# A mixture-of-experts loop: gate and up product as three fp32r products of high and low parts

## The chip, the cores and the metric

The kernel runs on one core of a Trainium2 chip. The metric is the device time of one execution in microseconds (us), start of the program to its end. The engines are PE (TensorE, matrix products, with a queue of weight loads of its own, PEld), ACT (ScalarE), DVE (VectorE), POOL (GpSimd) and SP (SyncE, which here issues most transfers). Each runs its own list of instructions in order; they meet at semaphores. SBUF is the on-chip memory of 128 partitions, PSUM the memory that PE writes its products to. TensorE's clock has two levels, 2.4 GHz (a granted clock of 1.00 in the rows) and 1.2 GHz (0.50).

## The reference

A decoder of two layers on 2 x 1024 tokens of 256 values. The change touches the last part alone, the experts of the second layer. What they compute, cut to that:

```python
xn = layernorm(x, gamma, beta); xf = xn.reshape(2048, 256)
probs = clip(softmax(xf @ router_w.T), 1e-8, 1.0)
topk_p, topk_i = top_k(probs, 2)              # two of 8 experts for each token
for eid in range(8):
    xe = xf * dense_gate[:, eid:eid + 1]      # scaled rows
    gate, up = split(xe @ gate_up_w[eid].T, 2)    # 256 -> 2 x 512
    out = out + (silu(gate) * up) @ down_w[eid].T # 512 -> 256
x = layernorm(x + xn + out)
```

All is float32.

## The kernel before, in words

The kernel is a chain of stages: chunked attention, cross attention, the mxfp4 layer, causal attention, a second cross attention, and `stage_experts` (L2088). The weights of all experts lie in SBUF when the last stage begins (`ExpertWeights`, L2072): `gate_up` of 8 x 2 x 1024 columns, `down` of 8 x 4 x 256.

`stage_experts` has three blocks. The first normalises the tokens, writes them to DRAM (`xn_rows`), routes them, and sorts the 4096 choices into slots of 128 rows, each of one expert: 39 slots (`SLOT_TILES`, L57), whose expert numbers are in `expert`. It ends with two one-hot matrices on DVE (L2367) and the products `tile_values` on POOL (L2236) and DVE (L2380), from which PE sums the slots' tables (L2277).

The second block is the experts' loop (L2396 to L2511). Each engine has a `step` function, which `lagged` (L92) calls once a slot: it gives the step the number of the newest slot and of the slots one, two or more behind it, so that in one step an engine works on several slots. With `turns=True` it also passes the turn modulo 4. In a step

- POOL (L2404) multiplies the gathered rows of slot t by their gates (L2410), copies the next slot's token indices (L2415) and issues its gather (L2418), then, for the slot three behind t, copies the choice indices (L2423) and issues the scatter of the output rows (L2426). Each issue waits for the copy in front of it.
- PE (L2440) transposes the hidden rows of slot u2 (L2447), makes the gate and up product of slot u1 (L2454), transposes the rows of slot t (L2462), and makes the down product of u2 (L2468).
- ACT (L2478) applies Silu to the gate half of u1 (L2482), copies the transposed rows of t out of PSUM (L2487), and the output rows of u2 (L2492).
- DVE (L2499) copies the transposed hidden rows of u2 (L2504) and multiplies gate by up for u1 (L2509).

There is one buffer for each of these intermediate tiles; the order within a step is written out by hand, and a semaphore counts the slots for each. The gate and up product of 128 rows is four matmuls in float32, of two halves of 512 columns and two halves of 128 contraction rows each:

```python
for n in range(2):
    for k in range(KD):
        last = nc.tensor.matmul(core.ps_s[:, n * FF:(n + 1) * FF], rows_tr[:, k, :],
                                weights.gate_up[:, bass.ds(x, 1), k, n * FF:(n + 1) * FF]..., start=(k == 0), stop=(k == KD - 1))
```

In the trace a float32 matmul stands as two records, an fp32r matmul (the type float32r, which PE takes in one pass) as one. The number x of the slot's expert is read by PE's queue from SBUF into a register (`value_load`, L2437).

The third block adds the two output rows of each token and normalises.

Of the kernel before, what the change touches and what calls it, by code (L numbers as in the profile page):

```python
# [28 lines left out]
P = 128  # L29
# [2058 lines left out]
def stage_experts(core, weights):  # L2088
# [17 lines left out]
    with core.stage() as ctx:  # L2106
        scratch = core.shared[:].rearrange("p (t d) -> p t d", d=D)
        router = core.sb(ctx, "ex_router", [P, KD, EXPERTS])
        gamma_row, beta_row = (core.sb(ctx, f"ex_{n}_row", [P, D]) for n in ("gamma", "beta"))
# [3 lines left out]
        xn_tr = [core.sb(ctx, f"ex_xn_tr{i}", [P, BATCHED, KD, P]) for i in range(2)]  # L2113
# [14 lines left out]
        past = core.sb(ctx, "ex_past", [P, SLOT_COLUMNS, EXPERTS])  # L2128
# [7 lines left out]
        in_tile = core.sb(ctx, "ex_in_tile", [P, 2, TILES, SLOT_COLUMNS])  # L2136

        gate_parts = core.sb(ctx, "ex_gate_parts", [P, 2, 2, TILES])
        tile_values = core.sb(ctx, "ex_tile_values", [P, 2, TILES, 3, SLOT_COLUMNS], F32R)
# [3 lines left out]
        at_place = core.sb(ctx, "ex_at_place", [P, TILES, P], F32R)  # L2143
# [22 lines left out]
        rows_tr_ready, rows_tr_copied, gate_up_ready = sem("rows_tr_ready"), sem("rows_tr_copied"), sem("gate_up_ready")  # L2166
# [228 lines left out]

        with nc.Block() as block:  # L2396
# [35 lines left out]
            @block.tensor  # L2432
            def _(pe):
                pe.wait_ge(weights.loaded, 16 * weights.LOADS)

                def expert_of(s):
                    return pe.value_load(expert[0:1, s:s + 1] if isinstance(s, int) else expert[0:1, bass.ds(s, 1)],  # L2437
                                         min_val=0, max_val=EXPERTS - 1)

                def step(t, u1, u2):  # L2440

                    x, y = (None if i is None else expert_of(i) for i in (u1, u2))
                    if u2 is not None:
                        pe.wait_ge(hidden_ready, u2 + 1)
                        need(pe, hidden_tr_copied, u2)
                        for k in range(KF):
                            last = nc.tensor.transpose(core.ps_c[:, k * P:(k + 1) * P], hidden[:, k * P:(k + 1) * P], core.ident[:])  # L2447
                        last.then_inc(hidden_tr_ready, 1)
                    if u1 is not None:

                        pe.wait_ge(rows_tr_copied, u1 + 1)
                        for n in range(2):
                            for k in range(KD):
                                last = nc.tensor.matmul(core.ps_s[:, n * FF:(n + 1) * FF], rows_tr[:, k, :],  # L2454
                                                        weights.gate_up[:, bass.ds(x, 1), k, n * FF:(n + 1) * FF].rearrange("p a n -> p (a n)"),
                                                        start=(k == 0), stop=(k == KD - 1))
                        last.then_inc(gate_up_ready, 1)
                    if t is not None:
                        pe.wait_ge(row_ready, t + 1)
                        need(pe, rows_tr_copied, t)  # L2460
                        for k in range(KD):
                            last = nc.tensor.transpose(core.ps_q[:, k * P:(k + 1) * P], row[:, k * P:(k + 1) * P], core.ident[:])  # L2462
                        last.then_inc(rows_tr_ready, 1)
                    if u2 is not None:
                        pe.wait_ge(hidden_tr_copied, u2 + 1)
                        need(pe, down_copied, u2)
                        for k in range(KF):
                            last = nc.tensor.matmul(core.ps_y[:, 0:D], hidden_tr[:, k, :],  # L2468
                                                    weights.down[:, bass.ds(y, 1), k, :].rearrange("p a n -> p (a n)"),
                                                    start=(k == 0), stop=(k == KF - 1))  # L2470
                        last.then_inc(down_ready, 1)

                lagged(pe, SLOT_TILES, 2, step)

            @block.scalar
            def _(act):

                def step(t, u1, u2):  # L2478
# [15 lines left out]
                lagged(act, SLOT_TILES, 2, step)  # L2494

            @block.vector
            def _(dve):

                def step(t, u1, u2):  # L2499
                    if u2 is not None:  # L2500
# [10 lines left out]
                lagged(dve, SLOT_TILES, 2, step)  # L2511

# [158 lines left out]
```

## Time and profile before

| what | value |
|---|---|
| runs | 1430.58 us median of 3 (1429.42 to 1432.01) |
| the profiled execution | 1428.61 us, span 1426.9 us |
| mean granted clock | 0.93 |
| PE busy | 1213.3 us (85%) |
| PEld busy | 846.1 us (59%) |
| DVE busy | 779.6 us (55%) |
| ACT busy | 668.0 us (47%) |
| POOL busy | 583.1 us (41%) |
| gate/up records on PE (L2454) | 312, 143.4 us busy |
| down records on PE (L2468) | 312, 73.9 us busy |

The span runs from the first to the last instruction. The experts' loop lies between 1144 and 1386 us of it. A record's length on PE is modelled, and records overlap: how fast PE goes is to be read from the distance of their starts.

### The profile page before, as it was taken

How to read it: one execution, taken by the hardware profiler on the slowest of the kernel's cores; microseconds unless marked ns; L12 is line 12 of the kernel's file. 1: busy time of each engine (PE TensorE's matmuls, PEld its weight loads, DVE VectorE, ACT ScalarE, POOL GpSimd, SP SyncE). 2: the span in 40 equal slices, each digit the busy share in tenths (PEclk: the TensorE clock that was granted, in tenths of full speed). 3: DMA queues.
4: the chain of work that ended last, by engine and by line, in shares of the span. 5: the costliest groups of instructions: out<-in, count | busy, mean ns of one | idle time of the engine just before them, and what ended most of it. 6: DMA issues, size and time to landing. Idle time of an engine off the chain costs nothing. (4 is left out here: it accounts for less than half of the span.)

```text
span 1426.9 us, 24233 instructions
## 1 busy us (share of the span) xinstructions
PE 1213.3 (85%) x7903; PEld 846.1 (59%) x7904; DVE 779.6 (55%) x1427; ACT 668.0 (47%) x1967; POOL 583.1 (41%) x664
## 2 busy tenths in 40 slices
PE   7888589565999999999899999998984279999970
PEld 4544367454666767776666777766764246666640
DVE  2587799783345556563455566656876612222215
ACT  2588357344556556655555566643661012222212
POOL 1255357557335324313643222102664245555535
PEclk9999689896899999999999999999995579999995
DMA  9000000010011010001100001007202001111105
GB/s 304 25 1 1 0 1 2 1 30 16 16 31 29 3 31 16 16 2 31 28 19 16 16 2 45 2 1 284 71 1 68 0 30 45 48 44 47 45 29 177
DMA packets 36134, 56.02 MB, mean 39 GB/s; under 512 B 6528, under 2 KB 27392, under 8 KB 36032
## 3 DMA queue, kind: packets, MB, share of 16 engines
q1 hardware_dynamic: 32288, 44.47, 10.5%
q0 software_dynamic: 3744, 10.23, 2.2%
q8 instruction: 59, 0.97, 0.3%
q14 instruction: 43, 0.35, 0.1%
HBM read 34.90 MB, written 9.31 MB: 31 GB/s over the span
## 5 line engine op out<-in xcount | busy, mean ns | idle before, releaser
L2016 DVE TENSOR_REDUCE ga_neg_top<-ps 128x1 f32<-128x128 f32 (+7 forms) x256 | 182.1, 753 | 195.0 <-PE ps L1786 194.6
L1897 ACT ACTIVATE ga_e<-ps,ga_neg_top 128x128 f32<-128x128 f32 (+7 forms) x256 | 188.2, 743 | 7.5 <-DVE ga_neg_top L2016 6.8
L1906 ACT COPY ga_e_tr<-ps 128x512 f32<-128x512 f32 (+3 forms) x192 | 92.1, 479 | 174.3 <-PE ps L1795 171.4
L1795 PE MATMUL ps<-ident,ga_e 128*128 128x128 f32 x1152 | 165.2, 279 | 0.9 <-DVE ga_e_tr L2024 0.8
L1811 PE MATMUL ps<-ga_e_tr,ga_v 128*64 128x256 f32 x1152 | 151.7, 391 | 4.1 <-ACT ga_att L1914 4.1
L2454 PE MATMUL ps<-ex_gate_up,shared 128*128 x312 | 143.4, 603 | 0.5 <-ACT shared L2487 0.5
L1795 PEld LDWEIGHTS ps<-ident,ga_e 128*128 128x128 f32 x1152 | 123.3, 142 | 28.1 <-ACT ga_e L1897 14.7
L2024 DVE COPY ga_e_tr<-ps 128x128 f32<-128x128 f32 (+3 forms) x192 | 106.0, 552 | 35.0 <-PE ps L1795 34.7
L1971 POOL TENSOR_TENSOR ga_q_lo<-shared,ga_q_hi 128x1024 fp32r<-128x1024 f32 x15 | 35.5, 2369 | 175.6 <-ACT ga_q_hi L1887 175.6
L2509 DVE TENSOR_TENSOR shared<-shared,ps 128x512 f32<-128x512 f32 x39 | 26.8, 687 | 137.0 <-ACT shared L2482 137.0
L1811 PEld LDWEIGHTS ps<-ga_e_tr,ga_v 128*64 128x64 f32 x1152 | 72.4, 136 | 49.0 <-issue 23.3
L2454 PEld LDWEIGHTS ps<-ex_gate_up,shared 128*128 128x128 f32 x312 | 57.3, 194 | 58.6 <-issue 58.6
L818 POOL TENSOR_TENSOR xa_e<-xa_e,xa_recip 128x1024 f32<-128x1024 f32 x32 | 60.9, 1902 | 69.7 <-DVE xa_recip L938 69.7
L2482 ACT ACTIVATE shared<-ps 128x512 f32<-128x512 f32 x39 | 23.3, 597 | 137.6 <-PE ps L2454 137.6
L1783 PE MATMUL ps<-ga_k_hi,ga_q_hi 64*128 64x512 f32 (+3 forms) x384 | 79.3, 409 | 4.1 <-PEq L158 2.3
L493 ACT ACTIVATE ca_e<-ps,ca_neg_top 128x64 f32<-128x64 f32 x256 | 75.9, 360 | 0.2 <-DVE ca_neg_top L524 0.2
L2468 PE MATMUL ps<-ex_down,shared 128*128 x312 | 73.9, 380 | 1.0 <-DVE shared L2504 1.0
L1957 POOL TENSOR_TENSOR shared<-shared,ga_cos 128x1024 f32<-128x1024 f32 x18 | 42.7, 2370 | 74.8 <-DMA shared<-shared 71.0
L1247 PE MATMUL ps<-x_tr,wide_weights 128*128 128x128 f32 x512 | 66.9, 286 | 2.0 <-ACT ga_e_tr L1906 2.0
L1783 PE MATMUL ps<-ga_k_lo,ga_q_hi 64*128 64x512 f32 (+3 forms) x384 | 67.7, 348 | 0.0
L1783 PE MATMUL ps<-ga_k_hi,ga_q_lo 64*128 64x512 f32 (+3 forms) x384 | 67.6, 348 | 0.0
L1247 PEld LDWEIGHTS ps<-x_tr,wide_weights 128*128 128x128 f32 x512 | 62.7, 200 | 8.2 <-issue 5.8
(321 smaller groups left out, 2533.8 us busy)
## 6 DMA issues: line engine op xcount, KB each, us to landing
shared<-shared SPq DMA_DIRECT2D x80, 128.0 KB, 2.4
ex_gate_up<-in_ex_gate_up SPq DMA_DIRECT2D x1, 8192.0 KB, 24.5
ex_down<-in_ex_down SPq DMA_DIRECT2D x1, 4096.0 KB, 35.8
x_tr<-in_x_tr SPq DMA_DIRECT2D x4, 512.0 KB, 7.0
x_nat<-in_x SPq DMA_DIRECT2D x1, 2048.0 KB, 11.7
xn_rows<-x_tr SPq DMA_DIRECT2D x8, 256.0 KB, 2.1
x_tr<-choice_rows SPq DMA_DIRECT2D x8, 256.0 KB, 5.0
shared<-choice_rows SPq DMA_DIRECT2D x8, 256.0 KB, 5.7
```

Source lines behind the costliest of these rows:

```text
L493: last = nc.scalar.activation(e[buffer][:, keys], ps_scores[buffer][:, keys], ACT.Exp, scale=SCALE, bias=neg_top[buffer][:, m:m + 1], accu ...
L818: nc.gpsimd.tensor_tensor(rows, rows, recip[:].unsqueeze(2).to_broadcast(by_head), ALU.mult).then_inc(weights_ready, 1)
L1247: last = nc.tensor.matmul(bank[:, g * P:(g + 1) * P], wq[:, k, block_of], x_tr[:, k, J * P:(J + 1) * P], start=(k == 0), stop=(k == KD - 1))
L1783: nc.tensor.matmul(ps_scores(t, half)[:, k0:k1], qs[J % 2][rows, c * R + r, :], ks[slot][rows, c, 0:k1 - k0], start=(i == 0), stop=(i == 2 ...
L1795: last = nc.tensor.transpose(ps_tr[n % 2][:, (kb - k0) * P:(kb - k0 + 1) * P], e[half][t % 2][:, kb * P:(kb + 1) * P], core.ident[:])
L1811: last = nc.tensor.matmul(ps_att[half * HD:(half + 1) * HD, :], v[:, v_slot(b, kb), kv * HD:(kv + 1) * HD], e_tr[g % 2][:, kb, half, :], s ...
L1897: nc.scalar.activation(e[half][t % 2][:, 0:blocks(t) * P], ps_scores(t, half), ACT.Exp, bias=neg_top[t % 2][:, half:half + 1], accum_out=s ...
L1906: nc.scalar.copy(e_tr[g % 2][:, k0:k1, half, t % 2 * P:(t % 2 + 1) * P], ps_tr[n % 2][:, 0:(k1 - k0) * P].rearrange("p (k t) -> p k t", t= ...
L2016: nc.vector.tensor_reduce(neg_top[t % 2][:, half:half + 1], ps_scores(t, half), AX.X, ALU.max, negate=True).then_inc(top_ready, 1)
L2024: nc.vector.tensor_copy(e_tr[g % 2][:, k0:k1, half, t % 2 * P:(t % 2 + 1) * P], ps_tr[n % 2][:, 0:(k1 - k0) * P].rearrange("p (k t) -> p k ...
L2454: last = nc.tensor.matmul(core.ps_s[:, n * FF:(n + 1) * FF], rows_tr[:, k, :], weights.gate_up[:, bass.ds(x, 1), k, n * FF:(n + 1) * FF].r ...
L2468: last = nc.tensor.matmul(core.ps_y[:, 0:D], hidden_tr[:, k, :], weights.down[:, bass.ds(y, 1), k, :].rearrange("p a n -> p (a n)"), start ...
```

## The change

The gate and up product is made as three fp32r products, high rows by high weights, high rows by low weights, low rows by high weights: 12 matmuls of 512 columns. The weights of the slot's expert are split in each step, one slot ahead: ACT copies them to `w_hi` in fp32r, DVE subtracts that from the weights to `w_lo`; there are two buffers of each, taken in turn. The transposed rows are split in the same way, by ACT's copy out of PSUM and a subtraction on DVE. The product's semaphore is split in two, after the gate half and after the up half. ACT and DVE read the slot's expert number themselves. To make room, buffers that only the first block uses are given back before the loop.

```diff
-        rows_tr = flat[:, 0:D].rearrange("p (k t) -> p k t", k=KD)
...
+        front_ctx.close()
+        loop_ctx = ExitStack()
+
+        def expert_at(engine, s):
+            return engine.value_load(expert[0:1, s:s + 1] if isinstance(s, int) else expert[0:1, bass.ds(s, 1)],
+                                     min_val=0, max_val=EXPERTS - 1)
+
+        w_hi, w_lo = ([core.sb(loop_ctx, f"ex_w_{n}{i}", [P, KD, 2 * FF], F32R) for i in range(2)] for n in ("hi", "lo"))
+        rows_hi, rows_lo = (core.sb(loop_ctx, f"ex_rows_{n}", [P, KD, P], F32R) for n in ("hi", "lo"))
...
     PE
                     if u1 is not None:
-                        pe.wait_ge(rows_tr_copied, u1 + 1)
-                        for n in range(2):
-                            for k in range(KD):
-                                last = nc.tensor.matmul(core.ps_s[:, n * FF:(n + 1) * FF], rows_tr[:, k, :],
-                                                        weights.gate_up[:, bass.ds(x, 1), k, n * FF:(n + 1) * FF].rearrange("p a n -> p (a n)"),
-                                                        start=(k == 0), stop=(k == KD - 1))
-                        last.then_inc(gate_up_ready, 1)
+                        buffer = (turn - 1) % 2
+                        pe.wait_ge(rows_lo_ready, u1 + 1)
+                        pe.wait_ge(w_lo_ready, KD * (u1 + 1))
+                        for n, ready in ((0, gate_half_ready), (1, gate_up_ready)):
+                            columns = slice(n * FF, (n + 1) * FF)
+                            for i, (rows, w) in enumerate(((rows_hi, w_hi), (rows_hi, w_lo), (rows_lo, w_hi))):
+                                for k in range(KD):
+                                    last = nc.tensor.matmul(core.ps_s[:, columns], rows[:, k, :], w[buffer][:, k, columns],
+                                                            start=(i == 0 and k == 0), stop=(i == 2 and k == KD - 1))
+                            last.then_inc(ready, 1)
                     if t is not None:
                         pe.wait_ge(row_ready, t + 1)
-                        need(pe, rows_tr_copied, t)
+                        need(pe, rows_lo_ready, t)
...
     ACT
+                def step(t, u1, u2, turn):
+                    if t is not None:
+                        x = expert_at(act, t)
+                        need(act, gate_up_ready, t - 1)
+                        for k in range(KD):
+                            nc.scalar.copy(w_hi[turn % 2][:, k, :], weights.gate_up[:, bass.ds(x, 1), k, :]
+                                           .rearrange("p a n -> p (a n)")).then_inc(w_hi_ready, 1)
                     if u1 is not None:
-                        act.wait_ge(gate_up_ready, u1 + 1)
+                        act.wait_ge(gate_half_ready, u1 + 1)
...
-                        nc.scalar.copy(rows_tr, core.ps_q[:, 0:D].rearrange("p (k t) -> p k t", k=KD)).then_inc(rows_tr_copied, 1)
+                        nc.scalar.copy(rows_hi[:], core.ps_q[:, 0:D].rearrange("p (k t) -> p k t", k=KD)).then_inc(rows_hi_ready, 1)
...
     DVE (behind the copy of hidden_tr)
+                    if t is not None:
+                        x = expert_at(dve, t)
+                        need(dve, gate_up_ready, t - 1)
+                        for k in range(KD):
+                            dve.wait_ge(w_hi_ready, KD * t + k + 1)
+                            nc.vector.tensor_tensor(w_lo[turn % 2][:, k, :], weights.gate_up[:, bass.ds(x, 1), k, :].rearrange("p a n -> p (a n)"),
+                                                    w_hi[turn % 2][:, k, :].bitcast(F32), ALU.subtract).then_inc(w_lo_ready, 1)
                     if u1 is not None:
                         dve.wait_ge(gate_ready, u1 + 1)
+                        dve.wait_ge(gate_up_ready, u1 + 1)
...
                         nc.vector.tensor_tensor(hidden, act_gate, core.ps_s[:, FF:2 * FF], ALU.mult).then_inc(hidden_ready, 1)
+                    if t is not None:
+                        dve.wait_ge(rows_hi_ready, t + 1)
+                        nc.vector.tensor_tensor(rows_lo[:], core.ps_q[:, 0:D].rearrange("p (k t) -> p k t", k=KD), rows_hi[:].bitcast(F32),
+                                                ALU.subtract).then_inc(rows_lo_ready, 1)
```

POOL's step is unchanged.

## Rows read from the trace of the kernel before

**Rows 1.** Busy time by stretch: from:to, length, busy us (instructions) of five engines, granted clock, DMA.

```profile
1200.00:1225.00 25.00, 25.00 (x94) 15.19 (x93) 6.10 (x9) 4.93 (x12) 12.99 (x23) 1.00 0.14 46
1150.00:1158.00 8.00, 6.86 (x10) 2.78 (x10) 0.43 (x1) 2.27 (x4) 2.82 (x4) 0.61 0.08 24
920.00:940.00 20.00, 20.00 (x156) 14.51 (x154) 11.94 (x14) 10.79 (x19) 0.00 (x0) 1.00 0.01 2
1135.00:1143.00 8.00, 4.55 (x21) 4.19 (x20) 3.18 (x6) 0.00 (x0) 0.00 (x0) 0.50 0.00 0
1085.00:1100.00 15.00, 11.73 (x56) 11.36 (x57) 14.79 (x21) 2.92 (x5) 8.57 (x7) 0.50 0.29 99
```

**Rows 2.** Timeline of one slot: start us, length us, engine, line, operation.

```profile
1239.85 0.60 PE L2447 MATMUL ps<-ident,shared 128*128 128x128 f32 x4
1240.13 0.37 ACT L2492 COPY shared<-ps 128x256 f32<-128x256 f32 x1 [1.08 <-PE ps L2468]
1240.29 3.60 PE L2454 MATMUL ps<-ex_gate_up,shared 128*128 x8
1240.64 0.69 DVE L2504 COPY shared<-ps 128x512 f32<-128x512 f32 x1 [1.14 <-PE ps L2447]
...
1243.72 0.38 PE L2462 MATMUL ps<-ident,shared 128*128 128x128 f32 x2
1243.92 0.60 ACT L2482 ACTIVATE shared<-ps 128x512 f32<-128x512 f32 x1 [3.42 <-PE ps L2454]
1244.55 0.69 DVE L2509 TENSOR_TENSOR shared<-shared,ps 128x512 f32<-128x512 f32 x1 [3.23 <-ACT shared L2482]
```

**Rows 3.** Timeline of POOL around the same slot.

```profile
1238.53 0.61 POOL L2410 TENSOR_TENSOR shared<-shared,ex_slot_gate 128x256 f32<-128x256 f32 x1 [0.96 <-PE ps L2462]
...
1242.38 1.01 POOL L2426 DMA_INDIRECT choice_rows<-shared,ex_tile_choice  x1 [0.82 <-POOL ex_tile_choice L2423]
1244.35 0.61 POOL L2410 TENSOR_TENSOR shared<-shared,ex_slot_gate 128x256 f32<-128x256 f32 x1 [0.96 <-PE ps L2462]
```

**Rows 4.** Timeline of PE and its loads: scores, router, slot sums, first slot.

```profile
932.59 0.39 PE L1783 MATMUL ps<-ga_k_hi,ga_q_lo 64*128 64x512 f32 x2
932.82 0.40 PE L1783 MATMUL ps<-ga_k_lo,ga_q_hi 64*128 64x512 f32 x2
...
1090.05 1.83 PEld L2259 LDWEIGHTS ps<-ex_router,ex_xn_tr 128*128 128x128 f32 x8
...
1138.26 3.49 PEld L2277 LDWEIGHTS ps<-ex_tile_values,ex_at_place 128*128 128x128 f32 x16 [2.56 <-DVE ex_at_place L2367]
...
1150.27 6.64 PE L2454 MATMUL ps<-ex_gate_up,shared 128*128 x8 [0.55 <-ACT shared L2487]
```

**Rows 5.** Groups by line and shape: busy us, mean ns of one, idle time before.

```profile
L1887 ACT CAST ga_q_hi<-shared 128x1024 fp32r<-128x1024 f32 x15 | 15.8, 1052 | 2.5 <-POOL shared L1959 2.5
...
L240 DVE TENSOR_TENSOR tail_z<-ps,tail_resid 128x256 f32<-128x256 f32 x32 | 13.1, 410 | 27.3 <-PE ps L1832 27.1
```

**Rows 6.** Single lines of the kernel: ns min/median/max, first and last start.

```profile
L1020 DVE TENSOR_TENSOR mx_x_scaled<-x_nat,mx_inverse x4: 1192/1192/1193, 261.2 to 312.9; 128x1024 f32<-128x1024 f32 x4
...
L2437 PEldq TENSOR_LOAD <-ex_expert x78: 295/302/493, 1149.1 to 1375.8; - x78
...
L2523 POOL TENSOR_TENSOR ex_rstd<-ex_var_eps,neg_half x8: 694/1113/1142, 1402.2 to 1420.9; 128x2 f32<-128x2 f32 x8
```

**Rows 7.** Timeline of POOL and DVE ahead of the loop.

```profile
1125.07 1.28 POOL L2236 TENSOR_TENSOR ex_tile_values<-ex_in_tile,ex_choice_iota 128x640 fp32r<-128x640 f32 x1 [21.92 <-DVE ex_in_tile L2367]
1125.26 3.23 DVE L2367 TENSOR_TENSOR ex_at_place<-ex_place_f,ex_place_iota 128x2048 fp32r<-128x2048 f32 x1
1126.31 3.30 POOL L2236 TENSOR_TENSOR ex_tile_values<-ex_in_tile,ex_gate_parts 128x640 fp32r<-128x640 f32 x1
...
1135.92 2.29 DVE L2367 TENSOR_TENSOR ex_at_place<-ex_place_f,ex_place_iota 128x2048 fp32r<-128x2048 f32 x1 [3.82 <-PE ps L2277]
```

More of the change, by code:

```diff
@@ L2112, in stage_experts @@
         var_eps, rstd, neg_mean, offset = (core.sb(ctx, f"ex_{n}", [P, TILES]) for n in ("var_eps", "rstd", "neg_mean", "offset"))
-        xn_tr = [core.sb(ctx, f"ex_xn_tr{i}", [P, BATCHED, KD, P]) for i in range(2)]
         logits, probs = (core.sb(ctx, f"ex_{n}", [P, TILES, EXPERTS]) for n in ("logits", "probs"))
@@ L2142, in stage_experts @@
         tile_choice, tile_token = (core.sb(ctx, f"ex_tile_{n}", [P, 1], I32) for n in ("choice", "token"))
-        at_place = core.sb(ctx, "ex_at_place", [P, TILES, P], F32R)
+        front_ctx = ExitStack()
+        tile_values = core.sb(front_ctx, "ex_tile_values", [P, 2, TILES, 3, SLOT_COLUMNS], F32R)
+        at_place = core.sb(front_ctx, "ex_at_place", [P, TILES, P], F32R)
+        gamma_row, beta_row = (core.sb(front_ctx, f"ex_{n}_row", [P, D]) for n in ("gamma", "beta"))
+        past = core.sb(front_ctx, "ex_past", [P, SLOT_COLUMNS, EXPERTS])
+        in_tile = core.sb(front_ctx, "ex_in_tile", [P, 2, TILES, SLOT_COLUMNS])
+        xn_tr = [core.sb(front_ctx, f"ex_xn_tr{i}", [P, BATCHED, KD, P]) for i in range(2)]
         flat = scratch.rearrange("p t d -> p (t d)")
-        rows_tr = flat[:, 0:D].rearrange("p (k t) -> p k t", k=KD)
         act_gate, hidden = (flat[:, D + i * FF:D + (i + 1) * FF] for i in range(2))
@@ L2165, in stage_experts @@
         row_ready, token_ready, choice_ready = sem("row_ready"), sem("token_ready"), sem("choice_ready")
-        rows_tr_ready, rows_tr_copied, gate_up_ready = sem("rows_tr_ready"), sem("rows_tr_copied"), sem("gate_up_ready")
+        rows_tr_ready, rows_hi_ready, rows_lo_ready = sem("rows_tr_ready"), sem("rows_hi_ready"), sem("rows_lo_ready")
+        w_hi_ready, w_lo_ready = sem("w_hi_ready"), sem("w_lo_ready")
+        gate_half_ready, gate_up_ready = sem("gate_half_ready"), sem("gate_up_ready")
         gate_ready, hidden_ready = sem("gate_ready"), sem("hidden_ready")
@@ L2434, in _ @@
                 pe.wait_ge(weights.loaded, 16 * weights.LOADS)
[L2436 to L2442, printed above, removed]
+                def step(t, u1, u2, turn):
+                    y = None if u2 is None else expert_at(pe, u2)
                     if u2 is not None:
@@ L2471, in step @@
                         last.then_inc(down_ready, 1)
-                lagged(pe, SLOT_TILES, 2, step)
+                lagged(pe, SLOT_TILES, 2, step, turns=True)
             @block.scalar
             def _(act):
-                def step(t, u1, u2):
+                act.wait_ge(weights.loaded, 16 * weights.LOADS)
+                def step(t, u1, u2, turn):
+                    if t is not None:
[4 more added lines that the diff above has]
+                                           .rearrange("p a n -> p (a n)")).then_inc(w_hi_ready, 1)
                     if u1 is not None:
-                        act.wait_ge(gate_up_ready, u1 + 1)
+                        act.wait_ge(gate_half_ready, u1 + 1)
                         need(act, hidden_ready, u1)
@@ L2492, in step @@
                         nc.scalar.copy(rows_out, core.ps_y[:, 0:D]).then_inc(down_copied, 1)
-                lagged(act, SLOT_TILES, 2, step)
+                lagged(act, SLOT_TILES, 2, step, turns=True)
             @block.vector
             def _(dve):
-                def step(t, u1, u2):
+                dve.wait_ge(weights.loaded, 16 * weights.LOADS)
+                def step(t, u1, u2, turn):
                     if u2 is not None:
```

7 lines of the change are left out of this document (2 added, 5 removed).

## The prediction

> **What bounds the kernel now.** I read the busy time by stretch first. In the experts' loop PE is busy through the whole stretch at a granted clock of 1.00, the upper level (2.4 GHz), while DVE works 6.1 and ACT 4.9 of 25 us [rows 1]. PE's idleness is so low that its own instruction stream must set the pace; the timeline of one slot shows that stream [rows 2]. A slot is four hidden-row transposes, eight gate/up matmul records (four products, each float32 in two passes), two row transposes and eight down records. From the start of the gate/up records (1240.29) to the row transposes (1243.72) are 3.43 us, so 0.429 us for one record of 512 columns. The other three pieces are the rest of the period. The period is read from POOL's own order [rows 3]: its row product starts at 1238.53 and again at 1244.35, so 5.82 us a slot. Other work on PE is then 5.82 - 3.43 = 2.39 us.
>
> The same group shows something that the page's shares hide: POOL is nearly as long. From the start of its row product (1238.53) to the end of its scatter issue (1242.38 + 1.01 = 1243.39) it needs 4.86 us, and it waits for PE only 0.96 us. So whatever PE gains beyond 0.96 us a slot is lost at once, and so is any gain that POOL's own work eats by getting slower.
>
> **The change, part by part.**
>
> *Gate/up on PE.* Eight fp32 records become 12 fp32r records of 512 columns. The loop shows no fp32r matmul of 128 rows. Lower bound: 512 columns at one a cycle, 512/2.4 = 0.213 us. The scores' fp32r products of 512 columns start in pairs (two halves of 64 rows) every 0.23 us at clock 1.00 [rows 1, 4]; that is the upper bound, if the two halves run side by side. I take 0.218, near the lower end, because the pair has two weight loads to place and the new record one: 12 x 0.218 = 2.62 us, 0.81 less than 3.43. PE alone would then give 5.82 - 0.81 = 5.01 us a slot (bounds 4.95 and 5.15).
>
> Does the weight load stay hidden behind a stream? In the slot sums, fp32r with 128 rows and 120 columns, 16 loads take 3.49 us, at most 0.22 each; in the router, eight loads for 8 columns each take 1.83 us, at most 0.23 each, both at clock 0.50 (1.2 GHz) [rows 1, 4]. The 112 more columns would add 0.09 us each if load and stream followed one another; they add nothing. So I cost the loads at nothing; without that cover each costs about 0.11 us at the upper level.
>
> *High and low parts of the weights.* ACT gets two copies 128x1024 to fp32r, 1.05 us each [rows 5], DVE two subtractions 128x1024 with both inputs in SBUF, 1.19 us each [rows 6]. DVE also gets the low rows, 128x256, 0.41 us [rows 5]. With what stands in the slot now (Silu 0.60, two copies of 256 columns 0.37 each; hidden copy and product 0.69 each [rows 2]) ACT then holds 2.10 + 0.60 + 0.74 = 3.44 us, DVE 2.38 + 1.38 + 0.41 = 4.17 us. Both fit under 5.01. The expert's number, read on PE now at 0.30 us [rows 6], moves to ACT and DVE as well; it lies beside the operation in front, and I charge 0.1 us on ACT, between 0 (covered) and 0.5 (not covered, with its register work).
>
> *The new order on ACT and DVE.* ACT does the two copies before the Silu, DVE the two subtractions before the hidden product, so PE's next transposes stand behind them. From the end of a slot's down products the chain is: output rows start 0.28 us into the next transposes and take 0.37, register 0.1, first copy 1.05, two subtractions 2.38, hidden product 0.69, hand-over 0.05: 4.92 us, after which PE still has a whole 5.01 us slot to do before its next down products end. Two slots for 4.92 + 5.01, less than PE's own 10.02; with 0.5 for the register 10.33. So this chain gives 5.0 to 5.2 a slot, and alone would cost at most 0.15.
>
> The Silu may start after half of the gate/up records; that is no gain, since the hidden product behind it waits for the second half and for the subtractions.
>
> *What the subtractions do to POOL.* This is the term that decides. Ahead of the loop, a DVE operation with two SBUF inputs (the one-hot places, 2.29 us alone) took 3.23 us when a POOL product was under way, and the next POOL product took 3.30 us instead of 1.28 [rows 7]: one waits until the other is done. Small POOL operations wait too: the reciprocal root on 2 columns takes 0.69 us at the least and 1.11 in the median, where DVE's sum of two SBUF tiles (L2544) runs beside it [rows 6]. The hidden product has one input in PSUM and runs over POOL's row product (1244.55 against 1244.35) without making it longer than 0.61 [rows 2, 3]. So now nothing on DVE stands in POOL's way, and after the change 2.38 us a slot will.
>
> POOL has three short operations a slot (row product, two index copies) and two DMA issues. An operation that arrives while a subtraction runs waits 0.6 us in the mean (half of 1.19). With period T the chance is 2.38/T. If only the three are held, T = 4.86 + 3 x (2.38/T) x 0.6, which gives T = 5.62. If the two issues are held as well, five in place of three, T = 6.04. If nothing is held, POOL stays at 4.86 and PE decides. The trace has no issue beside such a DVE operation, so these are the bounds. I take the three: for them the rows speak directly.
>
> *Start, end, and the rest.* The first gate/up product runs at the low clock, 6.64 us in a stretch of mean clock 0.61 [rows 1, 4]; twelve records at twice 0.218 are 5.2, so 1.4 less, and the low rows put 0.45 in front of it: 1.0 less in all. The first slot's weights are split while the first gather is on its way. The last product has nothing behind it on DVE and gains the 0.81 in full. Buffers that move in SBUF and four more semaphores: nothing, or under 0.1 us at the stage's end.
>
> **Sum**, for the profiled execution (1428.61 us, span 1426.9): 38 x (5.82 - 5.62) = 7.6, plus 0.8, plus 1.0 = 9.4 less, 1419.2. The median of the three runs is 2.0 above that execution, so the same sum from there gives 1421.2. I say 1420.
>
> **Rivals.**
>
> *POOL is not held, PE and the ACT-DVE chain decide* (T = 5.1). For it: the shortest DVE and POOL operations in the loop never touched, and POOL's order may settle into the gaps between the subtractions. Against: they are back to back for 2.4 of 5.1 us, and POOL rests for only 0.24. 38 x 0.72 + 1.8 = 29.2 less: 1401 from the median. Chance 0.25.
>
> *POOL's DMA issues are held too, and POOL becomes longer than PE was* (slower). Place: the gather and the scatter issue, 1.01 us the scatter's [rows 3]. It decides as soon as POOL's waits exceed the 0.96 us that it has in hand. At T = 6.04: 38 x 0.22 - 1.8 = 6.6 more, 1437. If DVE must also stand still for each whole issue, its chain carries up to two of them every other slot, T near 6.5, 1455. For it: POOL has no slack worth naming. Against: an issue is no elementwise operation, and nothing shows it to read SBUF for long. Chance 0.22.
>
> The Trainium skill puts it so in "GPSIMD Engine Reference" (2. Architecture): all that POOL reads of SBUF comes over one physical port that it shares with VectorE. Taken to the letter, an issue too, which reads its 128 indices there, would be held, and this rival's sum would be the forecast; no row of this trace has the two side by side.
>
> *The weight loads are not hidden.* A record then costs 0.213 + 0.11 = 0.32, twelve 3.88 us, 0.45 more than now; 39 x 0.45 is 17.6 more, 1448. The loads of the slot sums speak against it. Chance 0.05.
>
> That last one is a rule of the Trainium skill: "TensorE: Matmul & The Clock Gate" (The mechanism) has loads overlap a running matmul only where the row group differs, which is not so for 128 rows. The rows of the slot sums and the router don't bear it out.
>
> *The change buys nothing that can be measured*: T between 5.79 and 5.94, POOL held a little more than I think. Chance 0.08, beside 0.40 for my own case.
>
> **How the numbers follow.** My own case covers T from 5.5 to 5.75, that is 1417 to 1426. The range reaches down to 1398 (nothing held, T = 5.03) and up to 1444 (issues held, T = 6.2); outside stay the unhidden loads and the whole standstill. Faster by over 0.2% (2.9 us, about what a measurement of this kernel can tell): 0.40 + 0.25 = 0.65. Within it 0.08, slower 0.22 + 0.05 = 0.27.
>
> **What would show it.** In the changed profile: the twelve records about 0.22 us apart (not 0.32); the row product of POOL, now always 0.61, spread up to 1.8, its index copies up to 1.4; subtractions of 1.19 us stretched where POOL was first; PE with gaps of some 0.6 us a slot, before the row transposes (waiting for POOL) or before the hidden transposes (waiting for DVE), still at clock 1.00; a period of 5.6. I am wrong if POOL's operations keep their lengths, or if the issues grow from 1.01.

## The result, and the profile after

| | before | after |
|---|---|---|
| device time, median (lowest to highest) | 1430.58 us of 5 (1429.2 to 1432.17) | 1422.01 us of 5 (1421.18 to 1422.48) |
| the profiled execution | 1428.61, span 1426.9 | 1422.48, span 1420.8 |
| mean granted clock | 0.93 | 0.929 |
| slot period in the steady part | 5.82 us | 5.57 us |

The change makes the kernel faster by 0.6%: ratio 0.9937, 95% interval 0.9924 to 0.995. The forecast was 1420.

First the page of the kernel after, the engines' busy times:

```profile
PE 1197.0 (84%) x8059; PEld 873.5 (61%) x8060; DVE 881.0 (62%) x1545; ACT 743.3 (52%) x2046; POOL 608.3 (43%) x664
```

DVE has 101 us more than before and ACT 75, most of it the two halves of the weights' split. POOL's list of instructions is the same, yet it is busy for 608.3 us instead of 583.1, and that is the first sign of what happened. The stretches of [rows 1], in the kernel after (from:to, length, busy us and instructions of PE, PEld, DVE, ACT and POOL, granted clock, DMA):

```profile
1200.00:1225.00 25.00, 24.14 (x119) 19.08 (x118) 18.13 (x24) 13.00 (x22) 16.49 (x24) 1.00 0.14 47
1150.00:1158.00 8.00, 6.24 (x16) 4.54 (x16) 2.85 (x4) 4.25 (x5) 3.35 (x6) 0.50 0.07 19
```

PE, which had no gap at all, now has 0.86 us of them in 25, and since its records overlap in this view the true gaps are longer. It no longer sets the pace. The timeline of one slot (start, length, engine, line; in brackets the idle time before and who ended it), to be laid beside [rows 2, 3]:

```profile
1239.59 0.70 POOL L2420 TENSOR_TENSOR shared<-shared,ex_slot_gate 128x256 f32<-128x256 f32 x1
...
1240.48 0.66 PE L2453 MATMUL ps<-ident,shared 128*128 128x128 f32 x4 [0.41 <-DVE shared L2535]
1240.53 0.19 POOL L2425 COPY ex_tile_token<-ex_token 128x1 int32 x1 [0.24 <-POOL shared L2420]
...
1240.89 0.72 PE L2463 MATMUL ps<-ex_w_hi,ex_rows_hi 128*128 128x512 f32 x2
1241.04 0.37 ACT L2508 COPY shared<-ps 128x256 f32<-128x256 f32 x1 [2.02 <-DMA choice_rows<-shared,ex_tile_choice]
...
1241.50 1.01 POOL L2428 DMA_INDIRECT shared<-xn_rows,ex_tile_token  x1 [0.79 <-ACT shared L2508]
...
1241.77 2.00 ACT L2493 CAST ex_w_hi<-ex_gate_up 128x1024 fp32r x2 [0.36 <-issue]
...
1242.52 0.20 POOL L2433 COPY ex_tile_choice<-ex_choice 128x1 int32 x1
...
1242.96 2.36 DVE L2528 TENSOR_TENSOR ex_w_lo<-ex_gate_up,ex_w_hi 128x1024 fp32r<-128x1024 f32 x2 [0.95 <-ACT ex_w_hi L2493]
...
1243.53 1.54 POOL L2436 DMA_INDIRECT choice_rows<-shared,ex_tile_choice  x1 [0.82 <-POOL ex_tile_choice L2433]
...
1243.73 0.38 PE L2470 MATMUL ps<-ident,shared 128*128 128x128 f32 x2
...
1245.09 0.70 POOL L2420 TENSOR_TENSOR shared<-shared,ex_slot_gate 128x256 f32<-128x256 f32 x1
1245.24 0.68 DVE L2535 TENSOR_TENSOR shared<-shared,ps 128x512 f32<-128x512 f32 x1
```

Read POOL's rows from top to bottom: 0.70, 0.24 of hand-over, 0.19, 0.79, 1.01, 0.20, 0.82, 1.54, and the next row product starts at 1245.09, 0.02 us after the scatter's issue has ended. There is no wait for anybody in it (before, 0.96 us for PE stood there). 5.50 us a slot are POOL's own order and nothing else. Two of its operations are longer than before: the scatter's issue, 1.54 instead of 1.01, and the row product, 0.70 instead of 0.61. Of the page's 25 us the 39 issues of the scatter, 1530 ns in the mean for 1011, are 20.2, the 39 row products 3.0, and two token copies and two gather issues near the loop's start most of the rest. The issue starts 0.57 us into the first of two subtractions (1242.96 to 1245.32), when 0.61 of its 1.18 us are left; 1.54 is that and 0.93. The row product starts 0.23 us before the second one ends, and is 0.09 longer.

PE's piece is as short as hoped: 1240.89 to 1243.73 are 2.84 us for twelve records (3.43 before). ACT's output copy waits 2.02 us for the landing of the previous scatter; behind it stand the weight copies, and behind those the subtractions.

That it is so in every slot is seen on the line of the scatter's issue (nanoseconds, least, median, most; then who waited):

```profile
L2436 POOL DMA_INDIRECT choice_rows<-shared,ex_tile_choice x39: 978/1533/1836, 1170.8 to 1379.0; - x39
...
  ACT shared L2508: 74.8, 35
...
DMA to landing us min/median/max: 2.4/3.0/3.3
```

The periods by the starts of the row product: 5.49, 5.49, 5.49 and 5.78, over and over; the long one is the slot in which the loop of four turns round. There the subtractions start at 1281.97 and the issue at 1282.27, 0.88 us before the first of them ends, and it takes 1.81, again that and 0.93:

```profile
1282.27 1.81 POOL L2436 DMA_INDIRECT choice_rows<-shared,ex_tile_choice  x1 [0.82 <-POOL ex_tile_choice L2433]
```

What is late there is ACT: its weight copies start 0.63 us behind the output copy instead of 0.36, and the subtractions stand behind them.

31 periods from 1189.30 to 1361.89 have the mean 5.57. In them the scatter's issue takes 1.61 in the mean, 0.60 more than before, and the row product 0.09 more.

**Where the time went.** From the first token copy on POOL to the last scatter issue (before 1143.97 to 1385.05, after 1145.73 to 1378.97) the loop shrank by 7.8 us. It consists of three parts: 31 steady periods times 0.25 give 7.8; the first seven periods together are 1.4 longer (39.2 instead of 37.9); the end, from the last row product to the last scatter issue, is 1.5 shorter (17.1 instead of 18.5). The profiled execution is only 6.1 shorter than the one before, because the loop started 1.8 us later in it. On POOL nearly all of that comes up between 281 and 290 us of the span, far ahead of the experts, where nothing was changed. In the profiled executions of the kernels below the first row product starts anywhere between 1147.2 and 1150.5 us, so the late start isn't the change's.

### The profile page after: what moved, and what is told of

It is laid out like the page before. It is cut to its first block and busy times, and to the rows that moved or that the text cites. A ratio compares the mean times of both kernels' runs of the same rounds, so it can differ in the third digit from the quotient of the medians.

```text
span 1420.8 us, 25057 instructions
## 1 busy us (share of the span) xinstructions
PE 1197.0 (84%) x8059; PEld 873.5 (61%) x8060; DVE 881.0 (62%) x1545; ACT 743.3 (52%) x2046; POOL 608.3 (43%) x664
## 5 line engine op out<-in xcount | busy, mean ns | idle before, releaser
L2528 DVE TENSOR_TENSOR ex_w_lo<-ex_gate_up,ex_w_hi 128x1024 fp32r<-128x1024 f32 x78 | 92.7, 1229 | 42.1 <-ACT ex_w_hi L2493 42.0
L2493 ACT CAST ex_w_hi<-ex_gate_up 128x1024 fp32r x78 | 77.9, 1046 | 50.5 <-PEq L2189 35.0
L2436 POOL DMA_INDIRECT choice_rows<-shared,ex_tile_choice x39 | 59.7, 1530 | 31.9 <-POOL ex_tile_choice L2433 31.9
L493 ACT ACTIVATION_READ_ACCUMULATOR ca_e<-ps,ca_neg_top 128x1 f32 x256 | 65.1, 255 | 0.0
```

Source lines behind the costliest of these rows:

```text
L493: last = nc.scalar.activation(e[buffer][:, keys], ps_scores[buffer][:, keys], ACT.Exp, scale=SCALE, bias=neg_top[buffer][:, m:m + 1], accu ...
L2493: nc.scalar.copy(w_hi[turn % 2][:, k, :], weights.gate_up[:, bass.ds(x, 1), k, :] .rearrange("p a n -> p (a n)")).then_inc(w_hi_ready, 1)
L2528: nc.vector.tensor_tensor(w_lo[turn % 2][:, k, :], weights.gate_up[:, bass.ds(x, 1), k, :].rearrange("p a n -> p (a n)"), w_hi[turn % 2][: ...
```

## The experiments

What was open: do the subtractions make POOL's operations longer, as the prediction had it, and is it this and nothing else that keeps the period at 5.57? Each kernel below is the changed one with a single edit, unless it is said otherwise. The edits are shown shortened: `...` and words stand for long expressions. A time without a range is that of one run. Seven runs of the kernel before on one chip lie between 1428.0 and 1432.9 us, so a difference of two or three microseconds says nothing by itself; the periods, read from each kernel's own trace, say more.

### One SBUF input instead of two

```diff
-nc.vector.tensor_tensor(w_lo[...][:, k, :], weights.gate_up[...], w_hi[...][:, k, :], ALU.subtract)
+nc.vector.reduce_sum(sums[:, k, :], w_hi[...][:, k, :] as 16 groups of 64, AX.X)      # from the third slot on
```

> From the third slot on, DVE sums the high weights (128x1024, one SBUF input) in place of the subtraction; ACT's copies and all waits stay; the low weights are then those of the first slots. Theory (POOL's own order is the period, 4.86 us plus what the subtractions hold it): scatter issue back from 1.5-1.8 to 1.01 us, row product from 0.70 to 0.61, POOL gets time in hand, period from 5.57 to 5.15-5.3 us, where PE or the chain from ACT over DVE decides; total near 1408. Rival (the chain output rows, weight copies, DVE, hidden product sets the pace by its lengths, the hold on POOL is a bystander): period stays at 5.5-5.6, since DVE is as long as before; total near 1422.

Measured: 1407.28 us (the kernel before 1431.88 on the same chip). POOL in one slot:

```profile
1243.12 1.01 POOL L2429 DMA_INDIRECT shared<-xn_rows,ex_tile_token  x1 [0.80 <-POOL ex_tile_token L2426]
...
1245.16 1.01 POOL L2437 DMA_INDIRECT choice_rows<-shared,ex_tile_choice  x1 [0.82 <-POOL ex_tile_choice L2434]
1246.45 0.61 POOL L2421 TENSOR_TENSOR shared<-shared,ex_slot_gate 128x256 f32<-128x256 f32 x1 [0.29 <-PE ps L2471]
```

and DVE in the same stretch:

```profile
1244.68 2.35 DVE L2533 TENSOR_REDUCE ex_sums<-ex_w_hi 128x16 f32<-128x1024 f32 x2 [0.59 <-ACT ex_w_hi L2494]
```

DVE is busy for as long as with the subtractions (2.35 for 2.36), at the same place, and the scatter's issue runs beside it in 1.01 us. The period falls to 5.16 to 5.19, with 5.45 at each turn of the loop, and POOL waits for PE again. So the hold isn't DVE being busy, not the new semaphores, and not ACT's copies.

The reduction differs from the subtraction in two things: it reads one SBUF input instead of two, and it writes 16 columns instead of 1024. That the writing isn't what holds POOL is seen in the kernel after itself:

```profile
1241.33 0.69 DVE L2522 COPY shared<-ps 128x512 f32<-128x512 f32 x1 [0.57 <-PE ps L2453]
...
1245.84 0.41 DVE L2538 TENSOR_TENSOR ex_rows_lo<-ps,ex_rows_hi 128x256 fp32r<-128x256 f32 x1
...
1246.03 0.18 POOL L2425 COPY ex_tile_token<-ex_token 128x1 int32 x1 [0.24 <-POOL shared L2420]
```

The gather's issue at 1241.50 starts during a copy that writes 512 columns to SBUF, and takes its 1.01. The token copy at 1246.03 starts during the subtraction of the low rows, the same operation with the same output type as the long ones, but with one of its inputs in PSUM, and takes its 0.18; both are so in 32 slots. What is left is the second SBUF input.

### No subtraction at all

```diff
-nc.vector.tensor_tensor(w_lo[...], ..., ALU.subtract).then_inc(w_lo_ready, 1)
+dve.sem_inc(w_lo_ready, 1)                                                   # from the third slot on
```

> From the third slot on DVE leaves the subtraction of the weights out (its semaphore is raised at once); PE's twelve records and ACT's copies stay. Theory: PE's own stream decides, 12 records of 0.228 and the rest, period 5.15-5.25 us, total near 1406. Rival (what PE needs for twelve records with their hand-overs is itself the 5.5): period 5.45-5.6.

Measured: 1402.57 us, period 5.155 in every slot, turns of the loop included. This is PE's own stream: it is busy for all of the 25 us from 1200 on, and POOL waits some 0.3 us a slot for it. Beside the previous run it prices DVE's chain at about 0.08 us a slot in the mean (5.24 there), nearly all of it in the long slot at the turn.

### The split without its product

```diff
-for i, (rows, w) in enumerate(((rows_hi, w_hi), (rows_hi, w_lo), (rows_lo, w_hi))):
-    for k in range(KD):
-        matmul(core.ps_s[:, columns], rows[:, k, :], w[buffer][:, k, columns])
+for k in range(KD):
+    matmul(core.ps_s[:, columns], rows_hi[:, k, :] as f32, weights.gate_up[:, x, k, columns])
```

> The product is made in eight float32 records as before the change (from the high rows alone), with all the splitting on ACT and DVE kept. Theory: PE is the bound again at 5.82 us, POOL's 4.86 plus up to 0.9 of holds stays under it: period 5.80-5.90, total 1429 to 1434; the scatter issue is still 1.3 us or more in most slots. Rival (DVE's subtraction in front of the hidden product adds to PE's order, or holds come on top): period 6.2 or more, total near 1445.

Measured: 1429.02 us (the kernel before 1431.88 on the same chip), period 5.82 in the mean (5.71 to 5.94). The groups of POOL from 1160 to 1370 us (busy us, mean ns):

```profile
L2436 POOL DMA_INDIRECT choice_rows<-shared,ex_tile_choice x35 | 57.8, 1652 | 28.7 <-POOL ex_tile_choice L2433 28.7
...
L2420 POOL TENSOR_TENSOR shared<-shared,ex_slot_gate 128x256 f32<-128x256 f32 x36 | 23.5, 652 | 9.9 <-PE ps L2469 7.2 <-DMA shared<-xn_rows,ex_tile_token 2.4
```

The hold is there in full (1652 ns for an issue in the mean), and costs nothing, for it eats only POOL's wait for PE, which was 0.96 us a slot and is now 0.2 in three slots of four. The same hold that is free under a float32 product is the bound under the fp32r one.

### A second buffer for the output rows

ACT's output copy waits two us a slot for the previous scatter's landing. This takes the wait away.

```diff
-                        need(act, scattered, 16 * u2)
-                        nc.scalar.copy(rows_out, core.ps_y[:, 0:D])
+                        need(act, scattered, 16 * (u2 - 1))
+                        nc.scalar.copy(rows_out[turn % 2], core.ps_y[:, 0:D])
     POOL: tile_choice twice as well, and in front of the scatter
+                        need(pool, scattered, 16 * u3)
```

> The output rows (and the choice indices) get a second buffer, so ACT's output copy no longer waits for the last scatter to land; POOL waits for that scatter just before the next issue. Theory (POOL's order with its holds is the period): the weight copies start some 0.5 us earlier, POOL is held elsewhere, period still 5.4-5.7 us, total 1418 to 1426. Rival (the landing, which the weight copies queue behind, is what costs the time): period 5.15-5.25 us, total near 1408.

Measured: 1434.57 us, 2.7 over the one run of the kernel before on the same chip, and outside every expectation. Against the 1422 of the changed kernel it is clearly slower, and its period is 6.05. A slot of POOL:

```profile
1241.40 1.01 POOL L2429 DMA_INDIRECT shared<-xn_rows,ex_tile_token  x1 [0.79 <-POOL ex_tile_token L2426]
1242.41 0.20 POOL L2434 COPY ex_tile_choice<-ex_choice 128x1 int32 x1
1243.51 1.01 POOL L2438 DMA_INDIRECT choice_rows<-shared,ex_tile_choice  x1 [0.90 <-POOL ex_tile_choice L2434]
1244.54 0.95 POOL L2421 TENSOR_TENSOR shared<-shared,ex_slot_gate 128x256 f32<-128x256 f32 x1
1245.72 0.89 POOL L2426 COPY ex_tile_token<-ex_token 128x1 int32 x1 [0.24 <-POOL shared L2421]
```

and of DVE:

```profile
1243.79 2.78 DVE L2530 TENSOR_TENSOR ex_w_lo<-ex_gate_up,ex_w_hi 128x1024 fp32r<-128x1024 f32 x2 [0.73 <-ACT ex_w_hi L2495]
```

The same two subtractions, in a window that ends before the second begins:

```profile
1243.79 1.23 DVE L2530 TENSOR_TENSOR ex_w_lo<-ex_gate_up,ex_w_hi 128x1024 fp32r<-128x1024 f32 x1 [0.73 <-ACT ex_w_hi L2495]
```

Now the subtractions start 0.28 us after the scatter's issue instead of 0.6 before it. The issue, being first, keeps its 1.01, and the first subtraction, begun while the issue was under way, its 1.23: neither holds the other. Two short operations behind the issue are held, the row product (0.61 to 0.95), which starts in the first subtraction, and the token copy (0.18 to 0.89), which starts in the second. The subtractions stretch from 2.36 to 2.78, and all 0.42 of it is in the second, which has to wait for the row product. POOL's order in this slot becomes 4.86 + 0.34 + 0.71 + 0.08 (the hand-over of 0.90) = 5.99, and the period is 6.05 in the mean. What is held is decided by the phase between the two engines, and the wait for the landing had kept a good one.

### Smaller pieces

```diff
-nc.vector.tensor_tensor(w_lo[...][:, k, :], ...)                     # 2 of 1024 columns
+for n in range(2):
+    nc.vector.tensor_tensor(w_lo[...][:, k, half], ...)              # 4 of 512
```

> Each subtraction cut into two of 512 columns (four a slot, 0.69 us each by the other 512-column operations). Theory (an issue waits for the subtraction under way and no further): the scatter issue shrinks from 1.5-1.8 to 1.1-1.6 us, DVE needs 0.4 us more, period 5.3-5.5 us, total 1412 to 1420. Rival (an issue needs the port free for its whole length, so four pieces hold it as long as two): scatter issue stays at 1.5 or more, period 5.6-5.8.

Measured: 1423.91 us (before 1429.24), above the theory's 1412 to 1420. The groups of POOL from 1160 to 1370 us (busy us, mean ns):

```profile
L2436 POOL DMA_INDIRECT choice_rows<-shared,ex_tile_choice x36 | 45.3, 1258 | 29.5 <-POOL ex_tile_choice L2433 29.5
...
L2420 POOL TENSOR_TENSOR shared<-shared,ex_slot_gate 128x256 f32<-128x256 f32 x36 | 28.3, 787 | 11.9 <-PE ps L2470 9.5 <-DMA shared<-xn_rows,ex_tile_token 1.9
```

The issue is held 0.25 us in the mean instead of the 0.55 of the changed kernel in the same window, as a wait for the piece under way would have it; the rival's issue of 1.5 or more isn't there. But four pieces cost more than two (mean 770 ns each, 3.1 for 2.46), the row product then falls into them (787 ns against 693), and in 14 of the 27 slots between 1189 and 1345 us PE waits up to 1.0 us for the hidden product behind them. The periods run between 5.16 and 5.87, 5.67 in the mean, longer than the 5.57 of the changed kernel and than the 5.3 to 5.5 that the theory had. Why single pieces took up to 1.6 us wasn't followed further.

### POOL's index copies moved to DVE

If POOL's order is the bound, it should be made shorter. The first try gave DVE the two index copies, with two buffers each; the second adds the second output buffer.

```diff
     DVE, ahead of the subtractions
+                    need(dve, scattered, 16 * (u1 - 1))
+                    nc.vector.tensor_copy(tile_choice[(turn - 1) % 2], column(choice, u1))
+                    dve.wait_ge(gathered, 16 * (t + 1))
+                    nc.vector.tensor_copy(tile_token[turn % 2], column(token, t + 2))
     POOL
-                        nc.gpsimd.tensor_copy(tile_token[:], column(token, g)).then_inc(token_ready, 1)
-                        nc.gpsimd.tensor_copy(tile_choice[:], column(choice, u3)).then_inc(choice_ready, 1)
```

> DVE copies the index columns for POOL's issues ahead of time into two buffers each (2 small copies a slot in front of the subtractions); POOL keeps row product and two issues. Nothing is left out of the computation. Theory (POOL's order plus holds is the period): POOL needs at least 0.4 us less and, if the 0.8 us in front of an issue are the wait for its index copy, 2 us less, so its holds no longer matter; period 5.2-5.3 us, as in the run with one SBUF input, total 1406 to 1411. Rival (any hold of DVE and POOL on one another lands on the chain ACT-DVE-PE, whoever is shorter): period 5.45-5.6, total 1420.

> The same with two buffers for the output rows, which alone made the loop slower (6.04 us a slot) by letting the row product and the token copy be held. Theory: with POOL short it no longer matters where POOL is held, period 5.15-5.25 us, total 1404 to 1409. Rival (POOL's operations stretch the subtractions instead, 2.78 for 2.36 us as in that run, and this lands on the chain over DVE): period 5.4-5.6, total 1418.

Measured: 1483.85 us (ratio to before 1.0373, 1.0353 to 1.0393) and 1485.42 (1.0396, 1.0376 to 1.0417), periods from 5.1 to 10 us in the steady part. The waits of the first of them, from 1170 to 1365 us (us in total, times, the longest):

```profile
POOL shared L2422 <- PE ps L2468: 82.6, 26, 6.0
PEld ps L2451 <- DVE shared L2544: 49.2, 17, 4.8
...
DVE shared L2529 <- DMA choice_rows<-shared: 35.2, 21, 4.0
```

The chain reads upwards: the DVE copy of the choice indices waits for a scatter to land, up to 4.0 us; the subtractions and the hidden product are queued behind it; PE waits for those, POOL for PE. Neither theory had reckoned with this wait. The run says nothing for or against the theory of the hold; it says that a landing wait must not stand in the queue of the engine that the others wait for. The second output buffer changes nothing in it.

### POOL's index copies done away with

The loop on POOL is written out, so that each gather and scatter takes its indices straight from its column of the tables. No other engine is touched.

```diff
-                        nc.gpsimd.tensor_copy(tile_token[:], column(token, g)).then_inc(token_ready, 1)
-                        pool.wait_ge(token_ready, g + 1)
                         nc.gpsimd.indirect_dma_start(tokens_in, None, xn_rows,
-                                                     bass.IndirectOffsetOnAxis(ap=tile_token[:], axis=0))
+                                                     bass.IndirectOffsetOnAxis(ap=column(token, g), axis=0))
...
-                lagged(pool, SLOT_TILES, 4, step)
+                for i in range(SLOT_TILES + 4):
+                    g, t, u1, u2, u3 = (i - j if 0 <= i - j < SLOT_TILES else None for j in range(5))
+                    step(g, t, u1, u2, u3)
```

(and the same for the scatter's copy of `choice`)

> The changed kernel, with POOL's part of the loop written out for the 39 slots, so that each gather and each scatter takes its indices from its own column of the index tables; the two index copies a slot and the handshakes behind them are gone, the same two issues and the same row product stay. Theory A (POOL's own order, made longer by the subtractions, sets the period of 5.57): POOL's order falls from 4.86 to about 3.9 us plus 0.7 of holds, 4.6, and PE's 5.16 (what the kernel without subtractions needed) becomes the bound, or the chain of ACT and DVE with 5.2 to 5.3: in all 1403 to 1410 us, POOL waiting for PE before the row product by 0.5 us or more, the scatter's issue possibly still held over 1.01. Theory B (the landing of the scatter behind ACT's output copy and the subtractions behind that set the period whatever POOL does): the period stays above 5.45 and the time at 1417 to 1423.

Measured: 1406.34 us median of 4 (1405.31 to 1407.97), ratio to the kernel before 0.984, 0.9824 to 0.9857. Theory A's range was 1403 to 1410. POOL in one slot:

```profile
1241.42 0.99 POOL L2425 DMA_INDIRECT shared<-xn_rows,ex_token  x1 [0.79 <-POOL shared L2420]
...
1242.71 1.01 POOL L2430 DMA_INDIRECT choice_rows<-shared,ex_choice  x1 [0.30 <-issue]
...
1244.63 1.16 POOL L2420 TENSOR_TENSOR shared<-shared,ex_slot_gate 128x256 f32<-128x256 f32 x1 [0.91 <-PE ps L2466]
```

ACT's weight copies in the next slot:

```profile
1247.31 2.00 ACT L2489 CAST ex_w_hi<-ex_gate_up 128x1024 fp32r x2 [0.64 <-issue]
```

and the busy times of the engines in the stretch of [rows 1] (columns as there):

```profile
1200.00:1225.00 25.00, 24.82 (x124) 20.32 (x123) 19.26 (x25) 15.19 (x24) 15.16 (x15) 1.00 0.16 52
```

The issue is now over before it can be held; the row product takes the hold in its place (0.95 to 1.56 instead of 0.61) and it doesn't matter, for POOL still waits 0.91 us for PE. The periods are 5.15, 5.55, 5.15 and 5.28, with the mean 5.28 against PE's own 5.155. The long one is again at the loop's turn: ACT's copies start 0.64 us behind the output copy instead of 0.34, the subtractions and the hidden product stand behind them, and PE waits for that product. The longest row product (1.56) is in the same slot because it meets the same late subtractions.

The same edit on the kernel before the change is the control:

> The same edit of POOL's order on the kernel before the change (float32 gate and up product). If PE's stream of 5.82 us a slot bounds that kernel, as the prediction read it, nothing moves but the first slots of the loop, where POOL was the longer one (gaps of 4.7 to 4.9 us): 1424 to 1431 us, period 5.82, and POOL's wait for PE grows from 0.96 to about 1.9 us. If POOL's order had a part in the 5.82, the period falls below 5.75.

Measured: 1428.37 us (before 1429.78 on the same chip); the period stays at 5.82, and

```profile
1244.99 0.61 POOL L2410 TENSOR_TENSOR shared<-shared,ex_slot_gate 128x256 f32<-128x256 f32 x1 [1.96 <-PE ps L2458]
```

POOL waits 1.96 us for PE where it waited 0.96 in [rows 3]: a whole microsecond a slot off POOL gives at most 1.4 us in all there (one run, within the spread of the kernel before), and 15.7 after the change (1422.01 to 1406.34, on two chips whose kernels before are 0.8 us apart). The bound has moved from PE to POOL.

## Why the prediction was right

**The size and the bound were right, the instruction that is held was not, and that the sizes agree so well is luck.** The step that decides was "T = 4.86 + 3 x (2.38/T) x 0.6, which gives T = 5.62". Measured are 5.50 in three slots of four and 5.57 in the mean. POOL's own order sets it, lengthened by the subtractions; the run with one SBUF input shows both halves of that. But the prediction took the three short operations to be held and the issues not ("I take the three: for them the rows speak directly"). In the steady part it is the other way round: the scatter's issue takes 1.53 in the median, the row product gains 0.09, and both index copies keep their 0.18 and 0.20. By the prediction's own words ("I am wrong if POOL's operations keep their lengths, or if the issues grow from 1.01") this half of it fell. 0.76 us of holds a slot were forecast; 0.60 of the issue and 0.09 of the row product came in the mean of the steady slots.

**The step that failed is the averaging.** "An operation that arrives while a subtraction runs waits 0.6 us in the mean", with a chance of 2.38/T for each, takes arrivals to be spread evenly. They aren't: the loop locks into a phase. The scatter's landing releases ACT's output copy, the weight copies (0.36 + 2.0 us) and the subtractions follow, and so the next scatter's issue starts 0.57 us after the first subtraction (0.30 at the loop's turn), every time. That the landing fixes this phase is read off the order of the rows and fits the run without that wait; no run moved the landing alone. One operation is hit with certainty, the others never. With another phase two are hit, the row product and the token copy (the second output buffer, 6.05), and with a third only the row product, where it costs nothing (the indices straight from the tables). The mean over chances came near because this phase happens to cost about as much; the prediction had no reason for that.

**The rival with the issues held** (1437) was right about the mechanism: an issue beside a subtraction waits. It was wrong in adding the hold to the other three, when the five together share one pair of subtractions. Its second half, DVE standing still for a whole issue, didn't show: in the run with the second output buffer the first subtraction starts 0.28 us after the issue and takes its 1.23. DVE does give way to POOL's row product there, by 0.42 us. What the rule in the Trainium skill, "GPSIMD Engine Reference" (2. Architecture), says of the shared port, read to the letter for an issue, the trace bears out for the scatter's (1.54 for 1.01), and with one input on DVE there was no hold at all (1.01). The gather's issue stayed at 1.01 in the steady part because no subtraction runs beside it; in the first slots, where one does, it is longer too:

```profile
1161.15 0.95 POOL L2425 COPY ex_tile_token<-ex_token 128x1 int32<-128x1 int32 x1 [0.17 <-POOL shared L2420]
1162.89 1.20 POOL L2428 DMA_INDIRECT shared<-xn_rows,ex_tile_token  x1 [0.79 <-POOL ex_tile_token L2425]
```

**The fp32r record**: 0.218 taken, 2.84/12 = 0.237 measured with the first pair, which is slower (0.56 for two); the others stand 0.455 apart in pairs, 0.228 each. PE's own stream is 5.155, not 5.01: 0.22 more for the twelve records and 0.07 less for the rest. The 0.228 lies at the prediction's upper bound (0.23), and it cost nothing, because PE is not the bound. At clock 0.50 the first product took 5.29 us (1152.42 to 1157.71) where 5.2 was forecast.

**The loads hide**: the records of 128 rows follow each other every 0.228 us, each with a load of its own (468 loads for 468 records), and not every 0.32. The rival at 1448 is out. The rule beside it, the Trainium skill's in "TensorE: Matmul & The Clock Gate" (The mechanism), that a load overlaps only where the row group differs, isn't borne out by these records.

**POOL not held, 1401**: that is what the kernel would take if the hold were absent, 1407.28 and 1402.57 in the two runs without it. The prediction put the ACT-DVE chain at 5.0 to 5.2; 5.24 in the mean was measured with one SBUF input. The weight copies waited 0.36 us behind the output copy for the register, where 0.1 was charged between 0 and 0.5.

**Start and end**: 1.0 less at the start was forecast. The first product gave its 1.35, but the first seven periods are 1.4 longer in all. Before, they were short (4.72, 4.78, 4.85), since POOL and the gather's landing set them and PE's product didn't; the prediction counted 38 equal periods of gain. Two of the same periods are now 5.64 and 5.81, with the held token copy and issue shown above. The last product gave 0.6, not 0.81 (2.84 for 3.44), and the whole end 1.5: two products, not one, lie between the last row product and the last scatter.

So the sum, term by term: steady slots 38 x 0.20 = 7.6 forecast, 7.8 measured in 31 periods; start 1.0 less forecast, 1.4 more measured; end 0.8 forecast, 1.5 measured. Together 9.4 forecast, 7.8 measured over the loop, 6.1 between the profiled executions (the late start of the loop), and 8.6 between the medians. Only the steady slots came as summed; the start was 2.4 off one way and the end 0.7 the other.

## What to carry to other kernels

Before moving work to an engine that looks idle, write down the full order of every engine in the loop with its hand-overs, not its busy share: POOL was 41% busy over the span and had 0.96 us of 5.82 to spare, and a float32 product had hidden that. In this loop a DVE operation with two SBUF inputs was paid by POOL as well; what it hits depends on the phase, so look for what fixes the phase, and take work out of the engine that pays rather than waits out of the others. Here ten lines on POOL, worth at most 1.4 us before the change, brought 16 after it: 1406 us.

## What the runs showed of the hardware

- A POOL DMA issue of an indirect transfer, 1.01 us alone, takes 1.5 to 1.8 us in the changed kernel when it starts during a DVE subtraction of 128x1024 with both inputs in SBUF. It does not when DVE reads one SBUF input, for the same 2.35 us. A POOL index copy of one column (0.18) that starts during one takes 0.89 to 0.95. A DVE subtraction or product with one input in SBUF and one in PSUM, or a copy out of PSUM, holds none of them (0.18, 0.61 and 1.01 in the changed kernel and the one with the float32 product).
- Between a subtraction and POOL's row product the later one waits. The product took what was left of the subtraction and 0.47 us: 0.23 left gave 0.70, 0.48 gave 0.95, 0.68 gave 1.16. The subtraction that came behind the product took 1.64 for 1.22.
- An issue that was 0.28 us ahead of the subtractions kept its 1.01, and the subtraction beside it its 1.23: an issue under way did not hold DVE there.
- The landing of a scatter of 128 rows is 3.0 us from its issue in the median (2.4 to 3.3).
- An issue whose indices come straight from a column of a 40-column table takes 0.99 to 1.01 us, as long as from a tile of its own. Without the copy in front it starts 0.30 us after the issue before it, where copy and hand-over took 0.20 + 0.82.
- fp32r records of 128x128 by 512 columns at a granted clock of 1.00: one every 0.228 us, with a new load each.
